# The same calls in another order: the hand-written programs of a pipelined decoder-layer kernel, permuted on all five engines

## The chip, the cores and the metric

The kernel runs on 1 core of one Trainium2 chip. The metric is the device time of one execution in microseconds (us). Before, the median of 3 runs was 291.18 us (291.09 to 291.26). The core has four compute engines and a queue engine: TensorE (PE; its weight loads are shown as PEld), VectorE (DVE), ScalarE (ACT), GpSimd (POOL) and SyncE (SP), which issues nearly all of the DMAs. Each works through its own list of instructions in order; between engines there are only semaphores.

## The reference, cut to what matters

A decoder layer over `x` (16 batches x 128 rows x 256) and a context (16 x 128 x 64). `ln` is layer normalisation without parameters, `bf` rounds to bf16, `mx` rounds each block of 32 values to 8 bits with a shared power of two.

```
q, k, v = x @ Wq.T, x @ Wk.T, x @ Wv.T
x1 = ln(x + (q * cumsum(k * v, rows) * sqrt(256)/128) @ Wo.T)

scores = q_head(x1) . k_head(ctx) / sqrt(8)      # 32 query heads over 8 key heads, 8 wide
x2 = ln(x1 + softmax(scores) @ v_head(ctx))      # keys and values are the context itself

xb = bf(x2)
h  = bf(ln(xb) * ln_w + ln_b)
h  = bf(mx(h) @ mx(W1).T + b1)                   # 256 -> 1024
h  = bf(gelu_tanh(h))
h  = bf(mx(h) @ mx(W2).T + b2)                   # 1024 -> 256
out = ln(x2 + bf(xb + h))
```

## The kernel before

The 16 batches are 8 pairs, p = 0 to 7; `b` is the batch within a pair. A pair goes through seven stages, and at any time several pairs are under way, each in another stage: p[0] to p[6] in the code are the pairs in stages 0 to 6.

- Stage 1: `kv_proj`, `q_proj` (from `xt_r`, the transposed input that POOL rounds and splits in `split_xt_high` and `split_xt_low`), `k_times_v`, `running_sum`, `out_proj`, then `residual1`, `moments`, `mean_var` and a normalisation to x1.
- Stages 2 and 3, attention, where most of the time goes. `x1T` transposes x1 on PE, and ACT copies it to `xT`. POOL's `keys(p, b, u)` spreads the context keys over the heads (`kbd`, 96 x 512 each). `scores_a(p, b, k)`, k = 0 to 7, are PE matmuls whose only use is the row maximum, which DVE's `maxima(p, b, k)` takes (a reduction of a 128 x 512 PSUM bank, L1343). `max_high`, `max_low`, PE's `maxT`, and a small DMA by SP (`max_rows`, `xT<-mT`, L399) bring the maxima into `xT` as extra rows. `scores_b(p, b, k)` (L2175) makes the scores again with the maximum taken off, ACT's `exps` (L878) exponentiates them, `weigh` (L2188) multiplies with the values, `denominators` and `attention` on DVE and `residual2` on POOL end it.
- Stage 4: `norm3` (DVE, L1381), `weight3` and `shift3` (POOL, L595 and L601), then `quantise_h(p, 0)` to `(p, 6)` (DVE, L1431 to L1444), `h_T`, `ffn_up`, `hidden`, `gelu`, and `quantise_g(p, b, 0)` to `(p, b, 9)` (DVE).
- Stages 5 and 6: `g_T` (PE, L2241), `ffn_down` (L2254), `ffn_out` and `residual3` (POOL, L607 and L614), the last norm and the store.

Each engine has one program made of three functions written by hand: `head()` (pairs 0 to 3 started, and the weights of the FFN quantised by `weight_maxima`, `weight_scales` and `quantise_weight` on DVE), `step(p, on)`, which is run four times with the seven stages on seven pairs, and `tail()`. The order of the calls in them is the only thing that sets the order on an engine. Each call waits on semaphores for its inputs and for its output buffer. The waits are counts, so they don't change when a call moves.

Two waits matter below. `keys(p, b, 0)` writes over what the pair before read, and so it waits for that pair's last `scores_b` of the same batch; `keys(p, b, 1)` behind it has no wait of its own:

```
                if later(p) and u == 0:
                    pool.wait_ge(s_sbm, 16 * (p - 1) + 8 * (b + 1))
```

And SP's `load_xt(1)` waits until DVE has used the first block (`sp.wait_ge(s_lo0, 1)`). `warm`, `warm_p` and `warm_last` on PE are matmuls of zeros (L2026) whose result nobody reads. Where a group of calls such as the norm of the last stage appears with a last argument 0 or 1, it is one batch of the pair.

Of the kernel before, what the change touches and what calls it, by code (L numbers as in the profile page):

```python
# [45 lines left out]
def decoder_kernel(nc: bass.Bass, x, xt, ctx3, ctxv, wkv, wq, wo, ln_wb, w1, bias, w2, tri, ident, diag, out):  # L46
# [17 lines left out]
    with ExitStack() as ctx:  # L64
# [286 lines left out]
        def _(sp):  # L351
# [54 lines left out]
            def head():  # L406
                load_xt(0)
                load_weight("diag")
                load_weight("ident")
                load_weight("tri")  # L410
                load_values(0)
                load_weight("wo")
                load_keys(0)
                load_xt(1)
                load_weight("w1")
                load_x(0)
                load_bias()
                load_weight("ln")
                load_weight("w2")
                load_values(1)  # L420
                load_x(1)
                load_xt(2)
                load_keys(1)
                load_keys(2)
                load_x(2)
                load_xt(3)
                load_values(2)
                max_rows(1, 0)
                max_rows(1, 1)
                load_x(3)  # L430
                load_keys(3)
                spread_bias()
                load_xt(4)
                max_rows(2, 0)
                load_values(3)
                load_keys(4)

            def step(p, on):
                if on[3]:
                    max_rows(p[3], 1)  # L440
                if on[0]:
                    load_xt(p[0])
                if on[1]:
                    load_x(p[1])
                    load_values(p[1])
                if on[2]:
                    max_rows(p[2], 0)
                if on[5]:
                    store(p[5])
                if on[0]:  # L450
                    load_keys(p[0])
# [16 lines left out]
        def _(pool):  # L468
# [148 lines left out]
            def head():  # L617
                values(0)
                keys_rounded(0)
                split_xt_high(1)  # L620
                split_xt_low(1)
                keys(0, 0, 0)
                keys(0, 0, 1)
                var_eps(0, mv1, ve1, s_mv1, s_ve1, 0)
                rstd(0, ve1, rs1, s_ve1, s_rs1, 0)
                split_xt_high(2)
                split_xt_low(2)
                keys(0, 1, 0)
                var_eps(0, mv1, ve1, s_mv1, s_ve1, 1)
                rstd(0, ve1, rs1, s_ve1, s_rs1, 1)  # L630
                keys(0, 1, 1)
                keys_rounded(1)
                var_eps(1, mv1, ve1, s_mv1, s_ve1)
                rstd(1, ve1, rs1, s_ve1, s_rs1)
                shift_product(1, mv1, rs1, nb1, s_rs1, s_nb1)
                shift(1 - 1, nb1, s_nb1)
                split_xt_high(3)
                split_x1_high(1, 0)
                split_x1_high(1, 1)
                split_x1_low(1)  # L640
                split_xt_low(3)
                split_bias()
                keys(1, 0, 0)
                keys(1, 0, 1)
                keys(1, 1, 0)
                var_eps(2, mv1, ve1, s_mv1, s_ve1)
                rstd(2, ve1, rs1, s_ve1, s_rs1)
                values(1)
                keys(1, 1, 1)
                shift_product(2, mv1, rs1, nb1, s_rs1, s_nb1)  # L650
                shift(2 - 1, nb1, s_nb1)
                residual2(0)
                split_x1_high(2, 0)
                split_x1_high(2, 1)
# [3 lines left out]
                shift(0, nb2, s_nb2)  # L658
                keys_rounded(2)
# [3 lines left out]
                weight3(0)  # L663
                keys(2, 0, 0)
                shift3(0)
                keys(2, 0, 1)
                split_xt_high(4)
                keys(2, 1, 0)
                keys(2, 1, 1)
                keys_rounded(3)  # L670
                values(2)
                split_xt_low(4)

            def step(p, on):
# [4 lines left out]
                if on[6]:  # L679
                    shift_product(p[6], mv4, rs4, nb4, s_rs4, s_nb4)  # L680
                    shift(p[6], nb4, s_nb4)
# [2100 lines left out]
```

## Time and profile before

| | |
|---|---|
| median of 3 runs | 291.18 us (291.09 to 291.26) |
| profiled execution, its own time | 292.19 us |
| its span, first to last instruction | 290.4 us |
| mean granted TensorE clock | 0.982 |
| head, first row maximum at | 21.45 us |
| the four steps, about | 84.7 to 203.0 us |
| tail, about | 203.0 to 290.4 us |

All stretches and starts below are from that one profiled execution. A timeline row gives the start, the busy time, the engine, the line, the operation with its output and inputs, how many instructions it stands for, and in brackets how long the engine had been idle and what released it. Consecutive rows of an engine may overlap a little, since one instruction starts before the last has ended.

### The profile page before, as it was taken

The numbers are of one execution on the slowest core, as the hardware profiler recorded it, in microseconds if no ns is written. First come the engines' busy times: TensorE is split into PE (matmuls) and PEld (weight loads), VectorE is DVE, ScalarE is ACT, GpSimd is POOL, SyncE is SP. The second block draws the span as 40 slices with busy tenths as digits, with TensorE's granted clock in tenths as the row PEclk, the third lists the DMA queues.
The fourth block names the chain that finished last, engine by engine and source line by source line (L and its number), as shares of the span: only waits on it lengthen the run. The fifth ranks groups of instructions, "written<-read, shape, count | busy, mean of one in ns | idle before, by whom it ended". The sixth has DMA issues, their size and how long they took to land.

```text
span 290.4 us, 5342 instructions
## 1 busy us (share of the span) xinstructions
PE 271.7 (94%) x1640; PEld 165.5 (57%) x1640; DVE 256.2 (88%) x678; ACT 226.4 (78%) x386; POOL 174.6 (60%) x253
## 2 busy tenths in 40 slices
PE   7899998999998999999989998999699989997799
PEld 3776755476565775667556756575346444543354
DVE  3489899996999799999999999989996998799982
ACT  5551768479997699988998899889998899875650
POOL 2737291687466687868786878667777353533321
PEclk9999999999997999999999999999959999999999
DMA  7930200002110020022002200210010000100111
GB/s 238 393 113 2 99 3 0 10 5 71 37 43 0 0 79 15 2 65 77 11 5 64 79 9 5 67 43 9 7 36 5 2 1 0 37 2 1 38 37 38
DMA packets 11053, 12.68 MB, mean 44 GB/s; under 512 B 3216, under 2 KB 8336, under 8 KB 10768
## 3 DMA queue, kind: packets, MB, share of 16 engines
q1 hardware_dynamic: 10592, 11.55, 12.5%
q10 hardware_dynamic: 432, 0.79, 0.7%
q8 instruction: 13, 0.21, 0.3%
q14 instruction: 16, 0.13, 0.2%
HBM read 9.84 MB, written 2.10 MB: 41 GB/s over the span
## 4 chain that ended last, share of the span: by engine, by line
PE 55%; DVE 25%; ACT 7%; issue 6%; POOL 3%; DMA 3%; DVEq 0%; POOLq 0%; ACTq 0%
PE bank L2141 8%; PE bank L2175 8%; PE bank L2188 5%; DVE nm L1343 5%; PE bank L2075 4%; PE bank L2026 3%; PE bank L2062 3%; PE bank L2254 3%; PE bank L2101 3%; DVE st L1298 3%; PE bank L2229 2%; PE bank L2088 2%; PE bank L2125 2%; PE bank L2196 2%; DMA xT<-mT 2%
## 5 line engine op out<-in xcount | busy, mean ns | idle before, releaser
L1343 DVE TENSOR_REDUCE nm<-bank 128x4 f32<-128x512 f32 x128 | 84.0, 678 | 3.0 <-PE bank L2141 2.6
L878 ACT ACTIVATE p_sb<-bank 128x512 f32<-128x512 f32 x128 | 72.2, 600 | 11.1 <-PE bank L2175 10.5
L2141 PE MATMUL bank<-kbd,xT 96*128 96x512 f32 x128 | 56.2, 470 | 2.2 <-ACT xT L849 1.5
L2175 PE MATMUL bank<-xT,kbd 104*128 104x512 f32 x128 | 53.4, 448 | 4.6 <-DMA xT<-mT 3.1
L557 POOL TENSOR_TENSOR kbd<-k3r,diag_sb 96x512 fp32r<-96x512 f32 x32 | 33.5, 1061 | 11.4 <-PE bank L2175 11.4
L2175 PEld LDWEIGHTS bank<-xT,kbd 104*128 104x128 f32 x128 | 24.7, 194 | 18.1 <-ACT p_sb L878 5.9
L2141 PEld LDWEIGHTS bank<-kbd,xT 96*128 96x128 f32 x128 | 24.6, 195 | 16.4 <-DVE nm L1343 9.3
L2188 PE MATMUL bank<-p_sb,va_sb 128*32 128x512 f32 x256 | 33.7, 616 | 0.0
L511 POOL TENSOR_TENSOR rs<-ve,nhalf 128x2 f32<-128x2 f32 (+1 forms) x36 | 26.1, 724 | 4.6
L506 POOL TENSOR_SCALAR ve<-mv 128x2 f32<-128x2 f32 (+1 forms) x36 | 8.4, 233 | 33.4 <-DVE mv L1304 31.7
L2062 PE MATMUL bank<-wkv_r,xt_r 128*128 128x512 f32 x84 | 23.7, 404 | 0.0
L892 ACT ACTIVATE y_sb<-bank 128x512 bf16<-128x512 f32 x32 | 19.1, 596 | 5.5 <-PE bank L2229 4.8
L849 ACT ACTIVATE xT<-bank 96x512 fp32r<-96x512 f32 x32 | 18.6, 585 | 5.5 <-PE bank L2125 5.4
L1298 DVE BATCH_NORM_STATS2 st<-r_sb 128x6 f32<-128x256 f32 x48 | 19.3, 416 | 0.6 <-POOL r_sb L614 0.3
L2125 PEld LDWEIGHTS bank<-idr,x 128*96 128x96 f32 x128 | 14.2, 164 | 9.5 <-DVE nm L1343 3.6
L2229 PE MATMUL bank<-w1T,hT 128*128 128x512 bf16 x64 | 19.1, 379 | 0.0
L2026 PE MATMUL bank<-zero_b 128*128 128x512 bf16 x80 | 18.9, 379 | 0.0
L902 ACT ACTIVATE gT<-bank 128x1024 bf16<-128x1024 bf16 x16 | 16.3, 1022 | 2.9 <-PE bank L2241 2.8
L607 POOL TENSOR_TENSOR s_sb<-y_sb,xb_all 128x512 bf16<-128x512 bf16 x7 | 8.3, 1183 | 16.8 <-ACT y_sb L933 16.8
L2125 PE MATMUL bank<-idr,x 128*96 128x128 f32 x128 | 17.5, 260 | 0.5 <-ACT xT L871 0.5
L2062 PEld LDWEIGHTS bank<-wkv_r,xt_r 128*128 128x128 f32 x84 | 15.7, 189 | 3.5 <-issue 0.3
L898 ACT ACTIVATE g_sb<-y_sb 128x1024 bf16<-128x1024 bf16 x16 | 16.9, 1057 | 0.4
(135 smaller groups left out, 619.6 us busy)
## 6 DMA issues: line engine op xcount, KB each, us to landing
xt_sb<-in_xt SPq DMA_DIRECT2D x8, 256.0 KB, 2.9
x_sb<-in_x SPq DMA_DIRECT2D x8, 256.0 KB, 2.9
out_dram<-o_sb SPq DMA_DIRECT2D x7, 256.0 KB, 2.2
k_sb<-in_ctx SPq DMA_DIRECT2D x8, 192.0 KB, 2.9
x_all<-in_w SPq DMA_DIRECT2D x1, 1024.0 KB, 5.2
w_raw<-in_w SPq DMA_DIRECT2D x1, 1024.0 KB, 7.3
p_sb<-in_wkv ACTq DMA_DIRECT2D x2, 256.0 KB, 4.1
cv_sb<-in_ctxv SPq DMA_DIRECT2D x8, 64.0 KB, 2.0
```

The lines of the kernel that those rows point to most:

```text
L511: gp.tensor_tensor(rs[:, part(b)], ve[:, part(b)], nhalf[:, part(b)], ALU.pow).then_inc(rs_ready, batches(b))
L557: gp.tensor_tensor(kbd[0:MR, b, u, :, :], k3r[:, b, u, :].bitcast(F32).unsqueeze(1).to_broadcast([MR, KU, P]), diag_sb[0:MR, :].unsqueeze( ...
L878: sc.activation(p_sb[:, k, :], bankB[k % 2][:, :], ACT.Exp, scale=SCORE_SCALE).then_inc(s_ex, 1)
L1298: ve.bn_stats(st[:, b, :], rows).then_inc(st_ready, 1)
L1343: ve.tensor_reduce(nm[:, b, u, g, :], bankA[(2 + k + 11 * b) % 2][:, :].rearrange("p (k t) -> p k t", k=KU), AX.X, ALU.max, negate=True).t ...
L2026: mm(bankB[0][:, :], zero_b[:, 0:P], zero_b[:, :], start=True, stop=True)
L2062: last = mm(bankP[b][:, :], xt_r[:, a, c, b, :], wkv_r[:, w, c, :], start=c == 0 and n == 0, stop=c == KC - 1 and n == len(PARTS) - 1)
L2125: last = mm(bk[0:MR, g * P:(g + 1) * P], x3[:, b, u, g, :, :].rearrange("p a r -> p (a r)"), idr[:, :], start=True, stop=True)
L2141: mm(bankA[(2 + k + 11 * b) % 2][:, :], xT[0:MR, b, u, g, :], kbd[0:MR, b, u, :, :].rearrange("r k t -> r (k t)"), start=True, stop=True). ...
L2175: mm(bankB[k % 2][:, :], kbd[0:MR + 2 * KU, b, u, kk, :], xT[0:MR + 2 * KU, b, u, :, :].rearrange("r g s -> r (g s)"), start=True, stop=Tr ...
L2188: last = mm(value_bank(p, b)[VW * k:VW * (k + 1), :], va_sb[:, at0:at0 + VW], p_sb[:, u * KU + k, :], start=u == 0, stop=u == U - 1, tile_ ...
L2229: last = mm(bk[:, :], hT[:, c, b, :], w1T[:, c, cols], start=False, stop=c == KC - 1)
```

## The change

Every engine's `head()`, `step()` and `tail()` contain the same calls as before, with the same arguments, in another order. Nothing else differs, but that the line numbers of the helpers move by a few (POOL's by 1, ACT's by 6, PE's by 4). The number of calls is (head, step, tail) SP 30, 7, 6; POOL 55, 30, 63; ACT 100, 45, 92; DVE 187, 75, 189; PE 168, 62, 162. The head is reordered from its first call on; the step in some ten places; the tail mostly in its first third and around the last pairs.

The diff, cut to what the prediction speaks of:

```diff
@@ SP, head @@
                 load_xt(0)
+                load_bias()
                 load_weight("diag")
+                load_keys(0)
+                load_x(0)
+                load_weight("wo")
+                load_xt(1)
                 load_weight("ident")
                 load_weight("tri")
+                load_weight("w2")
+                load_weight("w1")
...
@@ POOL, head @@
                 weight3(0)
+                shift3(0)
                 keys(2, 0, 0)
-                shift3(0)
...
@@ POOL, step @@
                     weight3(p[4])
+                if on[2]:
+                    keys(p[2], 0, 0)
+                if on[4]:
                     shift3(p[4])
                 if on[2]:
-                    keys(p[2], 0, 0)
                     keys(p[2], 0, 1)
+                if on[0]:
+                    split_xt_high(p[0])
                 if on[5]:
                     ffn_out(p[5])
                     residual3(p[5])
                 if on[0]:
-                    split_xt_high(p[0])
                     split_xt_low(p[0])
...
@@ ACT, head @@
                 first_high(2)
+                first_high(3)
+                v_copy(0, 0)
+                identities()
+                q_copy(0)
+                v_copy(0, 1)
                 diagonal_rows(0)
-                first_high(3)
-                identities()
-                v_copy(0, 0)
-                v_copy(0, 1)
-                q_copy(0)
+                weight_magnitudes(1)
+                v_copy(1, 0)
                 weight_magnitudes(0)
...
                 gelu(0, 1)
+                x1T(2, 1, 0)
+                x1T(2, 1, 1)
                 exps(2, 0, 0)
                 exps(2, 0, 1)
-                norm1(3, 0)
                 v_copy(4, 0)
                 exps(2, 0, 2)
-                x1T(2, 1, 1)
+                norm1(3, 0)
...
@@ DVE, head @@
                 k_times_v(0, 0)
+                q_times_sum(0, 0)
                 k_times_v(0, 1)
-                q_times_sum(0, 0)
+                residual1(0, 0)
+                moments(0, 0, r1_sb[:, 0, :], st1, s_r1, 2 * 0 + 1, s_st1)
+                mean_var(0, 0, st1, mv1, s_st1, s_mv1)
                 q_times_sum(0, 1)
-                residual1(0, 0)
+                weight_maxima(1, 0)
...
@@ DVE, step @@
                     maxima(p[3], 1, 5)
+                if on[4]:
+                    norm3(p[4], 0)
+                    norm3(p[4], 1)
                 if on[5]:
                     quantise_g(p[5], 1, 9)
-                if on[4]:
-                    norm3(p[4], 0)
-                    norm3(p[4], 1)
...
                     quantise_h(p[4], 1)
+                if on[3]:
+                    denominators(p[3], 0)
+                if on[4]:
                     quantise_h(p[4], 2)
...
-                if on[3]:
-                    denominators(p[3], 0)
...
@@ DVE, tail @@
-                quantise_g(4, 1, 9)
...
                 norm3(5, 1)
+                quantise_g(4, 1, 9)
                 quantise_h(5, 0)
@@ PE, step @@
                 if on[1]:
                     kv_proj(p[1], 1, 0)
                 if on[3]:
-                    scores_b(p[3], 0, 1)
+                    scores_a(p[3], 1, 1)
+                    scores_b(p[3], 0, 0)
+                    scores_a(p[3], 1, 2)
...
                     scores_a(p[3], 1, 6)
+                if on[1]:
+                    q_proj(p[1], 1)
+                if on[3]:
                     scores_a(p[3], 1, 7)
                     scores_b(p[3], 0, 7)
                 if on[5]:
                     g_T(p[5], 1)
-                if on[1]:
-                    q_proj(p[1], 1)
...
@@ PE, tail @@
                 scores_b(7, 1, 0)
+                g_T(5, 1)
+                values_back(7, 0)
+                scores_b(7, 1, 1)
...
```

**POOL in a step, from `weight3(p[4])` on.** `h_sb` is the FFN's normalised input, `kbd` the spread keys, `xt_r` the rounded input of pair p[0], `s_sb` and `r_sb` are `ffn_out` and `residual3`. Before:

```order
L595 TENSOR_TENSOR h_sb<-h_sb,lnwb_sb 128x512
L601 TENSOR_TENSOR h_sb<-h_sb,lnwb_sb 128x512
L557 TENSOR_TENSOR kbd<-k3r,diag_sb 96x512 x2
L607 TENSOR_TENSOR s_sb<-y_sb,xb_all 128x512
L614 TENSOR_TENSOR r_sb<-x_all,s_sb 128x512
L528 TENSOR_SCALAR xt_r<-xt_sb 128x512
L533 TENSOR_TENSOR xt_r<-xt_sb,xt_r 128x512
```

The same place after the change:

```order
L596 TENSOR_TENSOR h_sb<-h_sb,lnwb_sb 128x512
L558 TENSOR_TENSOR kbd<-k3r,diag_sb 96x512
L602 TENSOR_TENSOR h_sb<-h_sb,lnwb_sb 128x512
L558 TENSOR_TENSOR kbd<-k3r,diag_sb 96x512
L529 TENSOR_SCALAR xt_r<-xt_sb 128x512
L608 TENSOR_TENSOR s_sb<-y_sb,xb_all 128x512
L615 TENSOR_TENSOR r_sb<-x_all,s_sb 128x512
L534 TENSOR_TENSOR xt_r<-xt_sb,xt_r 128x512
```

One of the two `keys` now stands ahead of `shift3`, on which DVE's `quantise_h` waits, and `split_xt_high` stands ahead of `ffn_out`.

**PE near the end of the tail, from `g_T(7, 0)` on.** `gq` is the quantised hidden layer, `w2T` and `gT` the operands of `ffn_down`, `bias_h` its bias row, and the matmuls out of `zero_b` are the fillers. Before:

```order
L2241 MATMUL bank<-idb,gq 128x128 x8
L2026 MATMUL bank<-zero_b 128x512 x14
L2252 MATMUL bank<-bias_h,ones_b 128x256
L2254 MATMUL bank<-w2T,gT 128x256 x8
L2026 MATMUL bank<-zero_b 128x512 x6
L2241 MATMUL bank<-idb,gq 128x128 x8
L2026 MATMUL bank<-zero_b 128x512 x4
L2252 MATMUL bank<-bias_h,ones_b 128x256
L2254 MATMUL bank<-w2T,gT 128x256 x8
```

The same place after the change:

```order
L2245 MATMUL bank<-idb,gq 128x128 x8
L2030 MATMUL bank<-zero_b 128x512 x8
L2256 MATMUL bank<-bias_h,ones_b 128x256
L2258 MATMUL bank<-w2T,gT 128x256 x8
L2030 MATMUL bank<-zero_b 128x512 x10
L2245 MATMUL bank<-idb,gq 128x128 x8
L2030 MATMUL bank<-zero_b 128x512 x6
L2256 MATMUL bank<-bias_h,ones_b 128x256
L2258 MATMUL bank<-w2T,gT 128x256 x8
```

The same 24 fillers stand there, six fewer ahead of the first `ffn_down` and four and two more ahead of what follows.

## Rows read from the trace of the kernel before

**Rows 1.** windows of steps and tail: busy PE, PEld, DVE, ACT, POOL; clock; DMA share; GB/s

```profile
84.70:203.00 118.30, 113.41 (x710) 73.92 (x711) 113.10 (x297) 104.49 (x185) 87.08 (x120) 0.99 0.12 34
203.00:290.40 87.40, 78.91 (x468) 39.72 (x466) 72.92 (x214) 65.10 (x104) 38.25 (x62) 0.96 0.05 17
```

**Rows 2.** the page: the chain that ended last, by engine

```profile
PE 55%; DVE 25%; ACT 7%; issue 6%; POOL 3%; DMA 3%; DVEq 0%; POOLq 0%; ACTq 0%
```

**Rows 3.** timeline of DVE, 13 to 22 us

```profile
14.00 2.00 DVE L1263 TENSOR_TENSOR gz<-gz 128x1024 bf16<-128x1024 bf16 x2
...
21.45 0.69 DVE L1343 TENSOR_REDUCE nm<-bank 128x4 f32<-128x512 f32 x1 [0.41 <-PE bank L2141]
```

**Rows 4.** timeline of ACT and of SP's queue, 0 to 13 us

```profile
2.10 0.43 SPq L394 DMA_DIRECT2D tri_sb<-in_tri  x1
...
5.86 0.35 SPq L358 DMA_DIRECT2D xt_sb<-in_xt  x1
...
6.17 1.14 ACT L841 ACTIVATE kbd<-diag_sb 32x512 fp32r<-32x512 f32 x2
```

**Rows 5.** timeline of DVE and POOL around 42 us

```profile
41.16 0.67 DVE L1285 TENSOR_TENSOR wz<-w_raw,win 128x512 int16<-128x512 f32 x1
41.75 2.81 DVE L1285 TENSOR_TENSOR wz<-x_all,win 128x512 int16<-128x512 f32 x1
...
41.99 2.02 POOL L557 TENSOR_TENSOR kbd<-k3r,diag_sb 96x512 fp32r<-96x512 f32 x2
```

**Rows 6.** timeline of DVE, `quantise_h` of pair 0 and of pair 5

```profile
71.10 0.69 DVE L1431 TENSOR_REDUCE am<-h_sb 128x16 f32<-128x512 bf16 x1 [2.16 <-POOL h_sb L601]
...
220.06 0.69 DVE L1431 TENSOR_REDUCE am<-h_sb 128x16 f32<-128x512 bf16 x1 [2.87 <-POOL h_sb L601]
```

**Rows 7.** timeline of PE at the entry to the steps, then its stretch

```profile
89.52 0.73 PE L2141 MATMUL bank<-kbd,xT 96*128 96x512 f32 x2 [1.45 <-ACT xT L849]
...
90.00:93.40 3.40, 3.40 (x20) 2.96 (x18) 3.40 (x9) 2.04 (x5) 3.01 (x6) 0.56 0.00 0
...
95.66 0.69 DVE L1343 TENSOR_REDUCE nm<-bank 128x4 f32<-128x512 f32 x1 [0.97 <-PE bank L2141]
```

**Rows 8.** timeline of PE in the third step

```profile
146.15 0.50 PE L2175 MATMUL bank<-xT,kbd 104*128 104x512 f32 x1 [0.66 <-DMA xT<-mT]
```

**Rows 9.** timeline of POOL, 156 to 167 us

```profile
156.94 1.28 POOL L595 TENSOR_TENSOR h_sb<-h_sb,lnwb_sb 128x512 f32<-128x512 f32 x1 [1.38 <-DVE h_sb L1381]
...
159.67 2.04 POOL L557 TENSOR_TENSOR kbd<-k3r,diag_sb 96x512 fp32r<-96x512 f32 x2
162.77 1.16 POOL L607 TENSOR_TENSOR s_sb<-y_sb,xb_all 128x512 bf16<-128x512 bf16 x1 [1.06 <-ACT y_sb L933]
```

**Rows 10.** timeline of DVE, 159 to 167 us; the last row in the tail

```profile
159.74 0.69 DVE L1431 TENSOR_REDUCE am<-h_sb 128x16 f32<-128x512 bf16 x1 [0.55 <-POOL h_sb L601]
...
160.77 0.96 DVE L1436 TENSOR_SCALAR sc<-am 128x16 bf16<-128x16 f32 x1
...
163.25 0.96 DVE L1444 TENSOR_TENSOR hq<-z,sc 128x512 bf16<-128x512 bf16 x1
...
166.19 0.42 DVE L1298 BATCH_NORM_STATS2 st<-r_sb 128x6 f32<-128x256 f32 x1
166.71 0.18 DVE L1304 BATCH_NORM_AGGREGATE mv<-st 128x2 f32<-128x6 f32 x1
...
249.48 0.17 DVE L1436 TENSOR_SCALAR sc<-am 128x16 bf16<-128x16 f32 x1
```

**Rows 11.** timeline of DVE and PE, 247 to 282 us

```profile
247.97 0.36 DVE L1361 RECIPROCAL rden<-bank 128x32 f32<-128x32 f32 x1 [2.29 <-PE bank L2196]
...
276.36 3.18 PE L2026 MATMUL bank<-zero_b 128*128 128x512 bf16 x14
...
280.27 0.69 DVE L1444 TENSOR_TENSOR gq<-gz,sc 128x1024 bf16<-128x1024 bf16 x1
...
281.66 0.61 PE L2241 MATMUL bank<-idb,gq 128*128 128x128 bf16 x8
```

More of the change, by code:

```diff
@@ L1055, in step @@
                     norm4(p[6], 1)
+                if on[3]:
+                    exps(p[3], 0, 5)
+                if on[5]:
+                    gT_copy(p[5], 0)
                 if on[3]:
@@ L1706, in step @@
                     norm3(p[4], 1)
+                if on[5]:
+                    quantise_g(p[5], 1, 9)
                 if on[3]:
@@ L1857, in tail @@
                 attention(6, 1, 1)
+                mean_var(4, 1, st4, mv4, s_st4, s_mv4)
                 quantise_g(5, 0, 2)
@@ L1975, in tail @@
                 quantise_g(7, 0, 9)
+                quantise_g(7, 1, 0)
+                quantise_g(7, 1, 1)
                 moments(6, 0, r3_sb[:, 0, :], st4, s_r3, 2 * 6 + 1, s_st4)
[L1977 to L1981 removed]
                 quantise_g(7, 1, 2)
@@ L2450, in step @@
                 if on[3]:
-                    scores_b(p[3], 0, 0)
+                    scores_a(p[3], 1, 0)
+                    x1T(p[3], 1, 1)
                 if on[1]:
@@ L2478, in step @@
                 if on[3]:
+                    scores_a(p[3], 1, 5)
+                    scores_b(p[3], 0, 5)
+                    scores_b(p[3], 0, 6)
+                    weigh(p[3], 0, 0)
                     scores_a(p[3], 1, 6)
+                if on[1]:
+                    q_proj(p[1], 1)
+                if on[3]:
                     scores_a(p[3], 1, 7)
@@ L2501, in step @@
                     scores_a(p[2], 0, 0)
+                    scores_a(p[2], 0, 1)
                 if on[3]:
@@ L2626, in tail @@
                 scores_b(7, 0, 5)
-                scores_a(7, 1, 7)
+                warm_p(2)
                 scores_b(7, 0, 6)
                 warm_p(2)
+                scores_a(7, 1, 7)
+                warm_p(2)
                 scores_b(7, 0, 7)
+                g_T(5, 0)
                 weigh(7, 0, 0)
+                warm_p(2)
                 maxT(7, 1)
-                warm_p(2)
-                g_T(5, 0)
                 weigh(7, 0, 1)
                 scores_b(7, 1, 0)
+                g_T(5, 1)
+                values_back(7, 0)
+                scores_b(7, 1, 1)
                 warm_p(2)
-                scores_b(7, 1, 1)
-                g_T(5, 1)
                 scores_b(7, 1, 2)
-                warm_p(2)
+                ffn_down(5, 1)
                 scores_b(7, 1, 3)
-                values_back(7, 0)
-                ffn_down(5, 1)
                 scores_b(7, 1, 4)
+                ffn_down(5, 0)
                 scores_b(7, 1, 5)
-                ffn_down(5, 0)
+                weigh(7, 1, 0)
+                h_T(6)
                 scores_b(7, 1, 6)
```

756 lines of the change are left out of this document (360 added, 396 removed).

## The prediction

> **What bounds the kernel now.** I read the windows first. In the four steps PE is busy 113.41 of 118.30 us and DVE 113.10, so the two share the bound and neither has 5 us to give; ACT and POOL have slack. In the tail PE is busy 78.91 of 87.40 us, part of it fillers, and DVE only 72.92 [rows 1]. The chain says the same in another way: 55% of the span is PE, 25% DVE, 7% ACT, and 6% "issue" [rows 2]. An order can't make the busy time shorter (no instruction is removed), only the waits. So I went through the timelines of PE and DVE for idle time whose releaser is another engine, and through DVE for instructions that last longer than their like. Then I laid the new order over the measured times and asked at each such place what stands there now.
>
> **The change part by part.** The sum is made against the profiled execution's own time, 292.19 us, which is 1.01 above the median of 291.18; the difference is taken over to the median.
>
> *Start, to the first row maximum at 21.45 us [rows 3].* Before, DVE runs two `weight_maxima` in 2.00 us (from 14.00) ahead of the first `moments`; now `residual1`, `moments` and `mean_var` stand in front of them. ACT's two `diagonal_rows` instructions cost 1.14 us at 6.17 [rows 4] and stood ahead of the last rounding of the query weights; now one call is behind the copies and the other far back. The gain can't be the full 2.00 + 1.14, since the first `keys` and x1's transposes must be there too: I put it at 1.05 us, near the middle. Against it works SP: `tri` was issued at 2.10, and is now behind `load_xt(1)`, which waits for DVE and was issued at 5.86 [rows 4]; with one issue (0.43) between, and two to three us for landing, `tri` is there at about 9.6, where `running_sum(0)` would want it at about 10.4 if PE and DVE gain what is said above; both are my estimates. Bounds: -1.4 (everything follows) to +1.0 (`tri` is late).
>
> *A held instruction at 42 us.* One `quantise_weight` on DVE takes 2.81 us, while its neighbour of the same form takes 0.67; it ends with POOL's two `keys` (41.99, 2.02) [rows 5]. In the new order another instruction meets them. I take -0.5; the bounds are -2.1 (2.81 less 0.67) and +0.5. In the head six more DVE instructions than before stand right behind the one whose result they need; in a step such a pair leaves 0.10 us between its two (166.19 + 0.42 to 166.71) [rows 10], where others overlap slightly. 6 x 0.12 is 0.7 at most; +0.4, since some fall into waits.
>
> *`quantise_h(0, 0)`* waits 2.16 us for POOL [rows 6]. `shift3(0)` is now ahead of `keys(2, 0, 0)`. Part of it only moves the wait: -0.4 (0 to -1.0, one `keys`, half of the 2.04 in rows 9).
>
> *Entry to the steps.* ACT copied x1's last transpose behind three `exps`, so PE stood idle 1.45 us; right after it the granted clock was 0.56 from 90.00 to 93.40, that is mostly at 1.2 GHz instead of 2.4, and DVE then waited 0.97 us for PE [rows 7]. ACT now makes that copy first. I take -1.0, the size of DVE's wait; the bounds are 0 and -1.5.
>
> *The steps, four times.* (a) `denominators(p[3], 0)` moves among the first instructions of `quantise_h`, into a stretch whose end is set by POOL. (b) Three dependent pairs fewer, 3 x 0.12. (c) `scores_b(0, 0)` is now behind one more `scores_a`, so the wait of 0.66 us for the small DMA [rows 8] becomes about 0.35. (d) `norm3` is 0.6 us sooner, with `quantise_g(p[5], 1, 9)` behind it. (e) Against: one `keys`, 1.02 us (half of 2.04) stands ahead of `shift3`, so `quantise_h(0)`, which already waited 0.55 [rows 10], starts about 1.0 - 0.6 = 0.4 later. That costs nothing if `quantise_h` was being held up anyway: `L1436` takes 0.96 us against 0.17 when POOL is quiet, and `L1444` 0.96, which ends as POOL's `ffn_out` does (162.77 + 1.16 = 163.93) [rows 9, 10]; and `ffn_out` waits for ACT, not for DVE. Without this cover it costs 0.4 a step. Sum a step: 0.27 + 0.36 + 0.3 = 0.93 at most of which waits elsewhere eat a part; (b) and (c) lie on different engines and only the later one counts. I take -0.4 a step, -1.6 in all; bounds 0 and -2.6.
>
> A rule bears on (e) and on the 42 us. The Trainium skill, page "SBUF — State Buffer", section "Who interferes with whom", says that VectorE and GpSimd share one pair of ports as an exclusive lock: a VectorE copy or tensor_scalar in a fast mode, or one with two inputs in SBUF, stands still until the GpSimd instruction ends, and a reduction never does. The rows agree (2.81 against 0.67, 0.96 against 0.17 us). By that rule `split_xt_high`, which the change puts just ahead of `ffn_out`, can also hold one of `quantise_h`'s instructions, by less than its own length; counted in full that would make the steps' term about zero instead of -1.6.
>
> *Tail.* The wait of 2.87 us ahead of `quantise_h(5, 0)` [rows 6] now has `quantise_g(4, 1, 9)` in it, about -0.6, but the `mean_var` of stage 4 is later, +0.35. At 247.97 DVE waited 2.29 us for PE's `values_back(7, 0)` [rows 11], which now stands directly behind `g_T(5, 1)`: -0.85, as the wait for the other batch behind it stays. Near the end 14 fillers take 3.18 us, 0.23 each, ahead of `ffn_down(7, 0)`; now 8, and 10 where 6 were. `g_T(7, 1)` started at 281.66, 0.70 us after its input was ready (280.27 + 0.69) [rows 11]; the fillers ahead of it are now 18 where there were 20, so -0.4 to -0.7. Together -1.5; bounds -3 and +0.5.
>
> *What I did not see.* Nearly every call of the head moved, and waits of 0.5 to 1.5 us as at the entry appear wherever two engines' orders don't match. I allow +1.5.
>
> Sum: -1.05 - 0.5 + 0.4 - 0.4 - 1.0 - 1.6 - 1.5 + 1.5 = -4.15. On 292.19 that gives 288.0, and on the median 287.0 us.
>
> **The rivals.**
>
> A, the forecast: gains in all three parts, 287.0 us, own range 284.0 to 289.5.
>
> B: the steps don't gain. PE is busy 96% of them [rows 1], and what DVE saves it then waits for PE. For it: both engines are full, so a gain must come on both. Against: the 0.66 of rows 8 is on PE. Time: 287.0 + 1.6 = 288.6.
>
> C: everything found is given back by mismatched waits in the head, so that it ends at 291.2: the allowance would be 5.7 instead of 1.5, four waits like the 1.45 of rows 7. The port rule above, counted in full, gives 288.6 alone and so is in B.
>
> D, slower. In a step POOL's `keys(p[2], 0, 0)` waits for the last `scores_b(p[3], 0)` of PE, and `shift3` is now queued behind it, and with it DVE's `quantise_h`, and behind that `h_T` and the FFN. In the new order that `scores_b` stands behind `q_proj(p[1], 1)`, later than before. Measured POOL comes to it at 156.94 + 1.28 = 158.2; I reckon PE's last `scores_b` about 0.7 us after it was, just in time. Each us that it is later passes to DVE four times. From 4.15 / 4 = 1.05 us a step on it decides; at 1.5 us the kernel takes 287.0 + 6 = 293.0. For it: POOL's `keys` had no one waiting behind them before, PE has no slack in the steps. Against: DVE's stretch there has 0.79 us of held time to absorb.
>
> **How the numbers follow.** A has 0.54, B 0.20, C 0.08 and D 0.18. The predicted time is that of A, 287.0. The range goes down to 284.0, where start, entry, steps and tail come near their lower bounds together (about 0.07 below it), and up to 292.5, which takes in B, C and the milder half of D. A measurement of this kernel can tell about 0.2%, 0.58 us, from no change. Faster by more: A and B with a little of C, 0.75; within: most of C, 0.07; slower: 0.18.
>
> **What would show it.** In the new profile: first row maximum at about 20.4 us; no idle time of PE of over 1 us at the entry to the steps and no clock below 0.9 there; the same row of successive steps 29.2 us apart or less (118.30 / 4 = 29.6 now [rows 1]); DVE's wait for `h_sb` in a step below 1 us, and POOL not idle ahead of the first `keys` (if it waits there for PE over a us, D is right); the wait for `xT<-mT` on PE halved; at the end `g_T(7, 1)` sooner after its input. The prediction is wrong if the steps are longer apart than before, if `tri` holds up the first `running_sum`, or if the head shows new waits for SP's loads, which have changed places the most.

## The result: 6.4% slower, and the profile after

The changed kernel takes 310.29 us (median of 4 runs, 308.89 to 310.97) beside 291.22 us before (4 runs): 1.064 times as long, 95% interval 1.059 to 1.069. I had forecast 287.0 us. The profiled execution has a span of 308.2 us (290.4 before) and a mean clock of 0.961 (0.982).

Page of the changed kernel, busy time, its slices and the chain that ended last:

```profile
PE 280.2 (91%) x1640; PEld 169.8 (55%) x1640; DVE 264.1 (86%) x678; ACT 226.6 (74%) x386; POOL 177.6 (58%) x253
...
PEclk9999999999999799989999799979967999999999
...
PE 42%; DVE 35%; issue 10%; ACT 6%; POOL 3%; DMA 2%; ACTq 0%; DVEq 0%; POOLq 0%
```

The same instructions are busy 7.9 us longer on DVE and 8.5 on PE (256.2 and 271.7 us before). On the chain that ended last, PE has lost about what DVE and "issue" have won [rows 2]. So there are not only new waits: some instructions on DVE last longer than they did. The view that finds them is the groups of instructions by line. Of DVE in the changed kernel (count, busy us, mean ns of one, idle us before them):

```profile
L1353 DVE CAST mx<-nm 128x32 bf16<-128x32 f32 x12 | 12.0, 1002 | 0.2
L1357 DVE TENSOR_TENSOR mx<-nm,mx 128x32 bf16<-128x32 f32 x12 | 6.7, 560 | 0.2
```

The same two groups of the kernel before:

```profile
L1354 DVE TENSOR_TENSOR mx<-nm,mx 128x32 bf16<-128x32 f32 x12 | 3.6, 298 | 0.2
L1350 DVE CAST mx<-nm 128x32 bf16<-128x32 f32 x12 | 3.0, 254 | 0.2
```

These are `max_high` and `max_low`, tiny instructions that I had not looked at. Together they take 18.7 us in place of 6.6. These 12.1 us are more than the 7.9 that DVE is busier, so some other instructions became shorter. PE's `maxT` waits for them. An instruction that lasts longer than others of its shape, because another engine is at work, is called held below. Windows of the changed kernel, the steps and then one place in the second step (columns as in [rows 1]):

```profile
84.70:220.80 136.10, 121.73 (x717) 77.58 (x717) 122.81 (x303) 104.92 (x185) 88.74 (x120) 0.95 0.10 30
...
134.00:137.00 3.00, 0.52 (x5) 0.38 (x6) 2.96 (x3) 0.28 (x1) 2.76 (x3) 0.93 0.02 5
137.00:140.00 3.00, 3.00 (x16) 2.50 (x16) 1.19 (x3) 1.24 (x3) 0.00 (x0) 0.50 0.04 11
```

The place itself, timelines of POOL, DVE and PE, and at the end two equal groups of `ffn_down` on PE:

```profile
131.36 1.59 POOL L596 TENSOR_TENSOR h_sb<-h_sb,lnwb_sb 128x512 f32<-128x512 f32 x1 [0.92 <-DVE h_sb L1384]
132.91 1.03 POOL L558 TENSOR_TENSOR kbd<-k3r,diag_sb 96x512 fp32r<-96x512 f32 x1
133.91 1.26 POOL L602 TENSOR_TENSOR h_sb<-h_sb,lnwb_sb 128x512 bf16<-128x512 f32 x1
135.14 1.03 POOL L558 TENSOR_TENSOR kbd<-k3r,diag_sb 96x512 fp32r<-96x512 f32 x1
...
133.05 3.21 DVE L1353 CAST mx<-nm 128x32 bf16<-128x32 f32 x1
136.30 0.60 DVE L1357 TENSOR_TENSOR mx<-nm,mx 128x32 bf16<-128x32 f32 x1
...
140.09 0.36 DVE L1364 RECIPROCAL rden<-bank 128x32 f32<-128x32 f32 x1 [1.87 <-PE bank L2200]
...
136.96 0.32 PE L2157 MATMUL bank<-idb,mx 128*72 128x128 bf16 x1 [2.48 <-DVE mx L1357]
137.29 1.92 PE L2258 MATMUL bank<-w2T,gT 128*128 128x256 bf16 x8
...
140.37 1.04 PE L2258 MATMUL bank<-w2T,gT 128*128 128x256 bf16 x8
```

Read it from the top. `keys` (132.91) follows `weight3` (131.36 + 1.59 = 132.95) without a pause, then `shift3`, then the second `keys`. DVE's `max_high` comes at 133.05, finds POOL at work, and lasts 3.21 us, to the end of the third POOL instruction; in the other three steps it lasts 2.21 or 2.22, to the end of the second. PE waits 2.48 us for `maxT` (1.9 in the others), and behind `maxT` stand `ffn_down`, `values_back` and all the scores. Right after that wait the granted clock is 0.50 (1.2 GHz) for 3 us, and DVE's `denominators` waits 1.87 us for the `values_back` that is late. The steps are 33.9 us apart instead of 29.6.

The clock has a share of its own. It falls after the wait in the other three steps too (windows of the changed kernel):

```profile
100.00:104.00 4.00, 2.11 (x15) 1.38 (x12) 3.90 (x5) 1.56 (x5) 3.08 (x4) 0.81 0.00 0
168.00:174.00 6.00, 4.10 (x26) 3.30 (x22) 4.12 (x7) 1.77 (x5) 3.00 (x4) 0.73 0.02 5
203.00:210.00 7.00, 5.55 (x32) 4.77 (x33) 4.57 (x12) 3.10 (x7) 1.24 (x2) 0.76 0.02 5
```

Eight matmuls of `ffn_down` take 1.92 us at 137.29 and 1.04 at 140.37, when the clock is back. PE's four waits for `maxT`, 1.89, 2.48, 1.90 and 1.90 us, are 8.2 us, and PE's extra busy time over the whole span is 8.5 us. My estimate from these two sums is that about half of what the steps lost is the wait and half the slower PE behind it; no run divides them.

Where the 19 us are, by DVE's starts in both traces: the first `max_high` of a step is 0.55 us later than before, the last one (233.13 in place of 216.06, in the first part of the tail) 17.1, and the last `quantise_g` 18.3. That gives the head, the steps (with the first part of the tail) and the rest of the tail some 0.6, 16.5 and 1.2 us; the last stretch to the end of the span is 0.5 us shorter. The two spans differ by 17.8 us, the two medians by 19.1.

### The profile page after: what moved, and what is told of

Its sections match the earlier page's. It is cut to its first block, busy times and chain, and to the rows that moved or that the text cites. A ratio compares the mean times of both kernels' runs of the same rounds, so it can differ in the third digit from the quotient of the medians.

```text
span 308.2 us, 5342 instructions
## 1 busy us (share of the span) xinstructions
PE 280.2 (91%) x1640; PEld 169.8 (55%) x1640; DVE 264.1 (86%) x678; ACT 226.6 (74%) x386; POOL 177.6 (58%) x253
## 4 chain that ended last, share of the span: by engine, by line
PE 42%; DVE 35%; issue 10%; ACT 6%; POOL 3%; DMA 2%; ACTq 0%; DVEq 0%; POOLq 0%
PE bank L2179 6%; PE bank L2145 6%; DVE nm L1346 5%; PE bank L2258 4%; DVE mx L1353 3%; DVE st L1301 3%; PE bank L2105 3%; PE bank L2066 3%; DVE gq L1447 2%; PE bank L2079 2%; PE bank L2192 2%; DVE gz L1490 2%; DVE gz L1443 2%; DMA p_sb<-in_wq 2%; PE bank L2233 2%
## 5 line engine op out<-in xcount | busy, mean ns | idle before, releaser
L2179 PE MATMUL bank<-xT,kbd 104*128 104x512 f32 x128 | 54.1, 458 | 1.1 <-ACT p_sb L884 0.9
L558 POOL TENSOR_TENSOR kbd<-k3r,diag_sb 96x512 fp32r<-96x512 f32 x32 | 34.0, 1072 | 12.4 <-PE bank L2179 12.1
L2192 PE MATMUL bank<-p_sb,va_sb 128*32 128x512 f32 x256 | 34.7, 627 | 1.0 <-ACT p_sb L884 0.9
L507 POOL TENSOR_SCALAR ve<-mv 128x2 f32<-128x2 f32 (+1 forms) x36 | 9.4, 262 | 38.4 <-DVE mv L1307 37.2
L2066 PE MATMUL bank<-wkv_r,xt_r 128*128 128x512 f32 x84 | 24.7, 410 | 1.1 <-DVE r_sb L1324 1.1
L898 ACT ACTIVATE y_sb<-bank 128x512 bf16<-128x512 f32 x32 | 19.1, 596 | 4.2 <-PE bank L2233 3.4
L2258 PE MATMUL bank<-w2T,gT 128*128 128x256 bf16 x128 | 20.0, 309 | 0.0
L2129 PEld LDWEIGHTS bank<-idr,x 128*96 128x96 f32 x128 | 15.4, 175 | 6.9 <-issue 4.7
L2233 PE MATMUL bank<-w1T,hT 128*128 128x512 bf16 x64 | 19.1, 379 | 0.0
L2030 PE MATMUL bank<-zero_b 128*128 128x512 bf16 x80 | 19.1, 379 | 0.0
```

The source lines that it names most:

```text
L558: gp.tensor_tensor(kbd[0:MR, b, u, :, :], k3r[:, b, u, :].bitcast(F32).unsqueeze(1).to_broadcast([MR, KU, P]), diag_sb[0:MR, :].unsqueeze( ...
L2066: last = mm(bankP[b][:, :], xt_r[:, a, c, b, :], wkv_r[:, w, c, :], start=c == 0 and n == 0, stop=c == KC - 1 and n == len(PARTS) - 1)
L2129: last = mm(bk[0:MR, g * P:(g + 1) * P], x3[:, b, u, g, :, :].rearrange("p a r -> p (a r)"), idr[:, :], start=True, stop=True)
L2179: mm(bankB[k % 2][:, :], kbd[0:MR + 2 * KU, b, u, kk, :], xT[0:MR + 2 * KU, b, u, :, :].rearrange("r g s -> r (g s)"), start=True, stop=Tr ...
L2192: last = mm(value_bank(p, b)[VW * k:VW * (k + 1), :], va_sb[:, at0:at0 + VW], p_sb[:, u * KU + k, :], start=u == 0, stop=u == U - 1, tile_ ...
L2233: last = mm(bk[:, :], hT[:, c, b, :], w1T[:, c, cols], start=False, stop=c == KC - 1)
```

## The experiments

Each ratio is against the kernel before on the same chip, and the brackets are its 95% interval. The kernel before took 291.0 to 292.0 us on these chips, so a difference of under 1 us between times from two chips says little. "Apart" is the distance of `max_high(p, 1)` from step to step in the profile, (start in the fourth - start in the first) / 3: 29.59 us before, 33.91 after.

**One call put back in the changed kernel** (POOL, step):

```diff
                     weight3(p[4])
-                if on[2]:
-                    keys(p[2], 0, 0)
-                if on[4]:
                     shift3(p[4])
                 if on[2]:
+                    keys(p[2], 0, 0)
                     keys(p[2], 0, 1)
```

> The changed kernel with one call put back: in the step, POOL's keys(p[2], 0, 0) behind shift3 again. Theory G (gap): the two dependent POOL calls weight3 and shift3 left 0.15 us between them, in which DVE's max_high got the shared ports; with keys between them POOL's train has no gap, max_high lasts 2.2 to 3.2 us instead of 0.3 and PE waits 1.9 to 2.5 us for it, in each of four steps. Then about 10 us come back (2.5 x 4): 300 us, and max_high lasts 0.3 us. Theory N (norm3 earlier): POOL's calls now meet max_high because norm3 was moved ahead of quantise_g; then keys alone gives back one keys (1.0 us) x 4: 306 us, and max_high still lasts over 1 us. Theory D (denominators): the wait of 1.8 us for PE in front of the rest of quantise_h is the cost; then this run stays at 309 to 310 us.

Measured: 296.87 us (1.017, 1.015 to 1.020), 30.46 apart. `max_high` lasts 0.24 us again. One call of 1.03 us is 13.4 of the 19 us, more than the 10 us of theory G; theory N's 306 us and theory D's 309 are out. The clock is back as well: PE's 717 matmuls of the steps are busy 115.79 us at a clock of 1.00 (window 84.7 to 207.0 us), where the same number took 121.73 at 0.95 in the changed kernel. So some 6 us of the 13.4 may be PE's speed. Timelines of DVE and POOL in this run:

```profile
129.82 0.24 DVE L1351 CAST mx<-nm 128x32 bf16<-128x32 f32 x1
130.10 1.20 DVE L1355 TENSOR_TENSOR mx<-nm,mx 128x32 bf16<-128x32 f32 x1
...
128.14 1.59 POOL L596 TENSOR_TENSOR h_sb<-h_sb,lnwb_sb 128x512 f32<-128x512 f32 x1 [0.92 <-DVE h_sb L1382]
129.87 1.28 POOL L602 TENSOR_TENSOR h_sb<-h_sb,lnwb_sb 128x512 bf16<-128x512 f32 x1
```

`shift3` depends on `weight3`, so there are 0.14 us between them, and `max_high` slips in. `max_low` does not: it is held 1.20 us.

**`denominators(p[3], 0)` put back** on DVE behind `maxima(p[2], 0, 1)`, alone and with `keys`:

```diff
                     quantise_h(p[4], 1)
-                if on[3]:
-                    denominators(p[3], 0)
...
                     maxima(p[2], 0, 1)
+                if on[3]:
+                    denominators(p[3], 0)
```

> The changed kernel with denominators(p[3], 0) on DVE put back behind maxima(p[2], 0, 1) in the step. Theory D: 1.8 us x 4 come back, and a little for the clock: 302 to 303 us. Theory G: max_high is still held 2.2 us or more, and the wait of denominators was only PE's lateness after it; quantise_h goes on during PE's catching up, so 1 to 4 us come back: 306 to 309 us. Theory N: like G.

> Both of these put back in the changed kernel. Theory G: as with keys alone within 1 us, about 299 to 300 us, if the wait of denominators follows from max_high. If both have a price of their own, 10 + 7 less than 310: 293 us. Theory N: about 302 us.

Measured: 309.84 us (1.064, 1.061 to 1.067) and 297.74 (1.021, 1.019 to 1.024). The wait of `denominators`, 1.5 to 1.9 us in each step, is real, and taking it away gives back nothing that can be told: it is PE's lateness seen from DVE. Theory D falls. The 1 to 4 us that theory G expected back in the first of the two runs did not come either.

**The kernel before with one call moved** (`keys(p[2], 0, 0)` between `weight3` and `shift3`, nothing else):

> The kernel before with one call moved: in the step, POOL's keys(p[2], 0, 0) between weight3 and shift3. Theory G: max_high is held 2 us or more here too, PE waits for it: 291.2 + 8 to 10 = 299 to 301 us. Theory N (norm3 must be earlier for it): max_high comes when weight3 has just ended, keys holds it by 1.0 us at most, quantise_h starts 1 us later of which the held time takes most: 291 to 295 us. Theory D: 291 to 292 us.

Measured: 297.72 us (1.024, 1.021 to 1.028), 31.35 apart, between theory N's 291 to 295 and theory G's 299 to 301. Here `max_high` gets in and `max_low` is the one that is held, to the end of `shift3` (130.14 + 1.26):

```profile
128.99 0.30 DVE L1352 CAST mx<-nm 128x32 bf16<-128x32 f32 x1
129.32 2.24 DVE L1356 TENSOR_TENSOR mx<-nm,mx 128x32 bf16<-128x32 f32 x1
...
127.90 1.28 POOL L595 TENSOR_TENSOR h_sb<-h_sb,lnwb_sb 128x512 f32<-128x512 f32 x1 [1.38 <-DVE h_sb L1383]
129.14 1.04 POOL L557 TENSOR_TENSOR kbd<-k3r,diag_sb 96x512 fp32r<-96x512 f32 x1
130.14 1.26 POOL L601 TENSOR_TENSOR h_sb<-h_sb,lnwb_sb 128x512 bf16<-128x512 f32 x1
131.36 1.04 POOL L557 TENSOR_TENSOR kbd<-k3r,diag_sb 96x512 fp32r<-96x512 f32 x1
```

So the move alone costs 6.2 us without any of the other edits, a third of the whole; within the change it costs twice as much. `max_high` got in here although there is no pause: `weight3` ended at 129.18 and `keys` started at 129.14. DVE's instruction started at 128.99, while `weight3` still ran; in the changed kernel it started 0.14 us after `keys`.

**The order of the change, with the pause given back**: one wait for `weight3` in front of `keys(p[2], 0, 0)`.

> The changed kernel, order untouched, with one wait added: in the step POOL's keys(p[2], 0, 0) first waits until weight3 has ended, as shift3 did when it stood there. No order changes; only the 0.1 to 0.2 us between the two instructions come back. Theory G (it is the gap through which DVE's max_high and max_low took the shared ports): max_high, which is ready 0.1 us after weight3's end, gets in and lasts 0.3 us; max_low may be held by keys or not; at least half of what putting keys back gave (13.4 us) comes back: 297 to 304 us. Theory L (length: DVE meets any POOL instruction that runs then, and it is the keys instruction, 1.03 us, ahead of shift3 that costs): nothing comes back, 309 to 311 us.

Measured: 310.21 us, `max_high` 2.3 to 3.3 us. My expectation was wrong, and the trace of it says why:

```profile
132.08 1.03 POOL L558 TENSOR_TENSOR kbd<-k3r,diag_sb 96x512 fp32r<-96x512 f32 x1
...
132.10 3.33 DVE L1354 CAST mx<-nm 128x32 bf16<-128x32 f32 x1
```

`keys` now starts 0.08 us behind `weight3` (it ended at 132.00), and DVE's instruction starts 0.02 us after it. Whether a pause alone is enough stays open; what the run does show is that an added wait on POOL gives nothing while `max_high` is held. The next run took the overlap away altogether.

**The order of the change, with `keys` waiting for DVE's `max_low`:**

```diff
                 if on[2]:
+                    pool.wait_ge(s_ml, 2 * p[2])
                     keys(p[2], 0, 0)
```

> The changed kernel, order untouched, with one more wait: in the step POOL's keys(p[2], 0, 0) waits for DVE's max_low(p[3], 1). The run before showed that the gap behind weight3 comes back (0.08 us) but DVE's max_high was ready 0.02 us after keys had started, so it said little on the mechanism. Theory T (train: max_high, once it finds POOL at work on keys, is held to the end of two or three POOL instructions, since they follow each other without a pause, and PE waits for its result): here max_high and max_low find POOL standing, last 0.3 us each, PE's wait is gone, keys starts 0.7 us later than now, and most of the 13.4 us comes back: 296 to 300 us, though keys still stands ahead of shift3. Theory L (the cost is the 1.03 us of keys, and now 0.7 more, ahead of shift3 and so of quantise_h, h_T and the FFN; this was my rival D's consequence): 310 to 313 us.

Measured: 300.83 us (1.031, 1.026 to 1.036), 31.60 apart: an added wait makes the kernel 9.5 us faster. That is 0.8 us outside theory T's range and far from theory L's 310 to 313; of L's mechanism a smaller part is there. (The profiled execution was the fastest of five, 298.05 us.)

```profile
129.44 0.24 DVE L1354 CAST mx<-nm 128x32 bf16<-128x32 f32 x1
129.72 0.31 DVE L1358 TENSOR_TENSOR mx<-nm,mx 128x32 bf16<-128x32 f32 x1
...
130.10 1.04 POOL L558 TENSOR_TENSOR kbd<-k3r,diag_sb 96x512 fp32r<-96x512 f32 x1 [0.77 <-DVE mx L1358]
...
132.40 0.69 DVE L1435 TENSOR_REDUCE am<-h_sb 128x16 f32<-128x512 bf16 x1 [0.90 <-POOL h_sb L602]
```

Neither of the two is held, and what is left of the move is the plain queueing of `shift3` behind `keys`, with the 0.77 us that `keys` itself now waits: `quantise_h` waits 0.90 us where it waited for nothing in the changed kernel. By these runs a step has 33.91 - 31.60 = 2.3 us of holding, with the late and slower PE behind it. 31.60 - 30.46 = 1.1 us is queueing together with the added wait, which no run divides, and 30.46 - 29.59 = 0.9 us is something else.

**That something else**, with keys and denominators put back. First DVE's `norm3` behind `quantise_g(p[5], 1, 9)` again, as before the change:

> The changed kernel with keys and denominators put back (297.7 us before this) and with DVE's norm3 behind quantise_g(p[5], 1, 9) again in the step. With keys put back, max_low is still held 1.20 us by shift3 where it took 0.30 before the change, since norm3, and so weight3, is 0.7 us earlier and its end no longer meets max_high. Theory N2 (that costs the remaining 0.8 us a step): max_low takes 0.3 us and 3 us come back, 294.5 to 295 us. Rival P (the remaining 0.8 us a step are from PE's new order): no change, 297 to 298 us, though max_low is short again.

Measured: 296.66 us, 30.35 apart: `max_low` is short again (0.31), and 0.3 us a step come back (30.64 apart with only keys and denominators put back) of the 0.8 expected. The time lies outside both ranges. What stays is a wait on DVE:

```profile
DVE vh_sb L1315 <- ACT q_sb L862: 3.6, 4, 0.9
```

(four waits of 0.9 us of `q_times_sum` for ACT's `q_copy`). PE's whole step put back to the old order on top of it:

> The kernel of the run with keys, denominators and norm3 put back (296.7 us), with PE's step put back to the order of before as well; ACT, SP and the rest stay as in the changed kernel. There residual1 waits 0.6 us in each step, and the steps are 0.55 us longer than before. Theory P (PE's new order, with x1T(p[2], 1, 0) behind values_back, and scores_b(0, 7) later, costs it): steps 29.6 us again, 2 us less, 294.3 to 295 us. If it is ACT's order or denominators and DVE's other moves: 296 to 297 us.

Measured: 298.85 us (1.025, 1.019 to 1.031), 31.11 apart: worse, and outside both expectations. I read it so that PE's new order fits ACT's new order, and that one engine's old order among the others' new ones loses more than it gives; no run tests that reading. Then only `q_proj(p[1], 1)` behind `scores_b(p[3], 0, 7)` and `g_T(p[5], 1)` again, and the same move made in the kernel before:

> The kernel with keys, denominators and norm3 put back (296.7 us), and on PE in the step q_proj(p[1], 1) behind scores_b(p[3], 0, 7) and g_T(p[5], 1) again. In the trace of that kernel DVE's q_times_sum waits 0.90 us for ACT's q_copy, which stands behind the last exps and gT_copy, and these wait for scores_b(0, 7), which is 1.1 us later since q_proj is ahead of it. Theory Q (that one call): the wait of q_times_sum goes, steps are 29.6 to 29.8 us apart instead of 30.3, and 2 to 3 us come back: 293.7 to 294.7 us. Rival M (many small mismatches): 296 to 297 us.

> The kernel before with that one move alone: on PE in the step q_proj(p[1], 1) ahead of scores_a(p[3], 1, 7). Theory Q: scores_b(0, 7) is 0.9 us later, with it the last exps, gT_copy and q_copy on ACT and q_times_sum on DVE, and the steps are 0.6 us longer: 293 to 294.5 us. Rival M: 291 to 292 us.

Measured: 295.84 us, 30.18 apart, and 291.55 us (0.999, 0.997 to 1.002), 29.80 apart. The wait goes from 0.9 to 0.17 us and appears at 0.56 us in the other kernel, as theory Q says, but a step moves by 0.2 us only. Theory Q is right on the wait and wrong on its price (295.84 lies between its range and rival M's, 291.55 in rival M's). This call is a small part, and the remaining 0.6 us a step are not settled.

**Whole functions.** The changed kernel with the step of all five engines from before, and the kernel before with the new head alone:

> The changed kernel with the step of all five engines from before; the new head and tail stay. Theory S (the loss is in the step alone): steps 29.6 us apart; the head's end is 0 to 1.2 us later than before, the tail within 1.5 us: 290 to 294 us. If the rest of the 5 us that is left after keys comes from head and tail by themselves: 296 us.

> The kernel before with the head of all engines from the changed one; step and tail from before. My sum had -2.5 us for the head with the entry to the steps. In the changed kernel the first row maximum was 0.4 us earlier, but the first quantise_g 1.25 us later than before. If the head's gain is lost in its last part: 291 to 293 us. If the old step takes up what the head gives (the entry without the 1.45 us wait on PE): 289 to 290 us.

Measured: 294.34 us (1.009, 1.006 to 1.012), 29.60 apart, and 292.99 us (1.004, 1.001 to 1.006). By these medians the step has 16 of the 19 us, the head about 1, the tail about 1.4; the steps are 29.60 us apart again, as before the change.

**Terms of my sum by themselves.** ACT's `x1T(2, 1, 1)` early and the fillers 4, 5, 3:

> The kernel before with two of the change's edits by themselves, at two places far apart: ACT's copy x1T(2, 1, 1) directly behind gelu(0, 1) in the head (my entry term, -1.0), and at the end 4, 5 and 3 fillers where 7, 3 and 2 stood, as in the changed kernel (my filler term, -0.4 to -0.7; here 9 ahead of g_T(7, 1) where 10 were). If the entry term is right, the 1.45 us wait of PE at 89.5 us is gone and max_high(2, 1) comes 0.5 to 1.0 us sooner than 98.83; if the fillers are right, the last quantise_g to the end of the span is 0.2 us or more shorter. Both: 289.8 to 290.4 us. If what the entry gives is taken by the next wait: 291.

Measured: 290.91 us (0.998, 0.996 to 1.001), no change that can be told. `max_high(2, 1)` started at 98.95 (98.83 before, and the first row maximum was 0.11 later already): the entry gave nothing. PE's 1.45 us there became these two waits, and the clock from 90.00 to 93.40 was 0.60, as low as the 0.56 of [rows 7]:

```profile
89.76 0.62 PE L2241 MATMUL bank<-idb,gq 128*128 128x128 bf16 x8 [0.62 <-DVE gq L1444]
90.69 1.65 PE L2075 MATMUL bank<-xt_r,wq_r 128*128 128x256 f32 x6 [0.32 <-DVE kv_sb L1308]
```

The fillers did give something: last `quantise_g` to the end of the span went from 10.1 to 9.7 us. Then `shift3(0)` ahead of `keys(2, 0, 0)`, with 4, 3 and 2 fillers and three more at the very end:

> The kernel before with two small edits: in the head POOL's shift3(0) ahead of keys(2, 0, 0), and at the end 4, 3 and 2 fillers where 7, 3 and 2 stood, the other three behind ffn_down(7, 1). The fillers: g_T(7, 1) no longer waits behind them (it started 0.70 us after its input), so the end comes 0.5 to 0.7 us sooner against the last quantise_g. shift3: if DVE's wait of 2.16 us ahead of quantise_h(0, 0) is on the path, that call and all behind it come 0.7 to 1.0 us sooner, and the whole is 289.6 to 290.0 us; if only DVE's slack grows, the first quantise_g stays where it is and the whole is 290.5.

Measured: 292.24 us (1.003, 1.001 to 1.005), slower by a little, and outside both expectations. `quantise_h(0, 0)` came 1.02 us sooner and `maxima(2, 0, 0)` 0.04: DVE had slack there, the term is nothing. And something else now set the end of the span: DVE's last result came at 286.40 (288.09 before), PE's last filler at 289.76 (290.15 before). PE, then DVE:

```profile
282.69 7.07 PE L2026 MATMUL bank<-zero_b 128*128 128x512 bf16 x32
...
285.99 0.41 DVE L1421 TENSOR_SCALAR o_sb<-r_sb,mv,rs 128x256 f32<-128x256 f32 x1 [1.06 <-POOL rs L511]
```

The store that follows DVE's last result takes about 2.2 us, so it would be over at 288.6, and the fillers end at 289.76 of 290.0. So eight of the 16 closing filler calls were left out (nobody reads their result):

> The kernel with the two small edits (shift3(0) ahead of keys(2, 0, 0), three fillers moved behind ffn_down(7, 1)), and 8 of the 16 closing fillers left out (work whose result nobody reads). In that kernel PE's last filler ended at 289.76 of a span of 290.0, while DVE ended at 286.40 and the store behind it takes about 2.2 us. If the closing fillers set the end, the span is now set by the store, 1.2 to 1.4 us sooner: 290.9 us, or 0.1 to 0.7 us less than before. If the store or something else set it, nothing changes: 292.2 us.

Measured: 290.50 us, beside 291.35 before on that chip (0.997, 0.995 to 0.999): 0.3% faster than before and 6% faster than the change, the only kernel here whose interval lies below that of no change. It does less work than either, by the eight filler calls.

## Why the prediction was wrong, point by point

- **The step that failed is (e) of the steps' sum**: with one `keys` ahead of `shift3`, `quantise_h(0)` starts 0.4 us later, and "That costs nothing if `quantise_h` was being held up anyway". The sum took -1.6 us for the four steps; measured, they lost about 16. I followed the moved call to the DVE call that waits for its result, and not to the DVE calls that run at the same time. It set POOL's instructions one behind the other just when `max_high` and `max_low` come, which stand ahead of `quantise_h` and feed PE. This is shown by one call put back (-13.4 us), and by the wait that takes the overlap away and leaves the order (-9.5 us). In the kernel before, `max_high` (158.03) and `max_low` (158.35) passed where POOL's `weight3` had ended (156.94 + 1.28 = 158.22 [rows 9]) and `shift3`, which needs its result, had not begun (158.37). I first took this pause of 0.15 us for the cause. What the runs show is when `max_high` got in with `keys` close behind `weight3`: it did when it started 0.15 us ahead of `keys` (the run with one call moved), and not when it started 0.02 or 0.14 us after.
- **The rule was named and used on the wrong instructions.** I had the page "SBUF — State Buffer" of the Trainium skill, section "Who interferes with whom", in the text, and applied it to `quantise_h` and `split_xt_high`, not to `max_high` and `max_low` beside `keys`. By its rule a cast (`max_high`) can be held if its operands meet the conditions of a mode with two ports, and an instruction with two inputs in SBUF (`max_low`) while GpSimd reads SBUF. The rows agree: 3.21 and 1.02 us against 0.24 and 0.30. The page says that the engine that issues first has the ports for its whole instruction. Here the hold lasted over two and three POOL instructions that followed each other without a pause (2.22 and 3.21 us).
- **Rival D had the right side, and its mechanism is the smaller part.** `shift3` queued behind `keys` costs at most 1.1 us a step when `max_high` and `max_low` are not held. That PE's last `scores_b` would be late for `keys` did not happen: POOL does not wait ahead of `keys` at 132.91. I had given it 0.18 and a price from 1.05 us a step on; the real total is 4.3 us a step, and most of it was in none of my rivals. Of the cover that (e) counted on, `L1444` ended at 164.21, 0.28 after `ffn_out` (163.93), and not with it [rows 9, 10].
- **The order of events within the held stretch.** (d), `norm3` sooner, was counted as a small gain. It moved `weight3`'s end ahead of `max_high`, and cost 0.3 us a step with `keys` put back. The move of `keys` costs 6.2 us alone and 13.4 within the change; that `norm3` makes the difference is my reading of these runs, and no run tests these two edits by themselves.
- **(a) `denominators`**: not settled. With `keys` put back the kernel takes 296.87 us with the move and 297.74 without, with `keys` moved 310.29 and 309.84; in both pairs the intervals overlap. The 0.27 that my sum has for it stands on no row. **(c)** the mechanism was right: no wait for `xT<-mT` of the kind of [rows 8] is left in the changed trace; its gain is not seen, as DVE is later. **(b)**, the dependent pairs, has no run of its own.
- **Start, -1.05**: the first maximum came at 21.09 in the profile, 0.36 sooner; `tri` was not late (issued at 6.56, landed 3.1 us later, first `running_sum` at 12.16). The start scatters: it was 19.7 to 21.4 us in runs with the same head. I overlooked one more held instruction there: DVE's last rounding of the query weights (L1236) took 1.77 us at 8.09 beside POOL's preparation of the keys, and 0.69 before. It did so in four of the eleven profiles with the new head and in none with the old one; what it is worth is not shown, since the first maximum came at 21.37 in a profile without it. **42 us**: three `quantise_weight` instructions took 3.58 us from 40.91, about 1.5 more than three of 0.68; before, the held one was 2.1 too long. So the held time fell by about the -0.5 that I took, while POOL's two `keys` took 2.99 us there in place of 2.02. **`quantise_h(0, 0)`, -0.4**: its wait vanished, and by the run with `shift3(0)` moved that is worth 0.
- **Entry, -1.0**: worth 0; and in the changed kernel PE waits there again, for another copy, now behind `gelu(0, 1)`:

```profile
85.02 0.47 PE L2145 MATMUL bank<-kbd,xT 96*128 96x512 f32 x1 [1.21 <-ACT xT L855]
```

- **Tail, -1.5**: it is about 1.4 slower. The wait of 2.87 us is still 2.59 with `quantise_g(4, 1, 9)` in it, and all of it 1.2 us later, 0.4 of it from before the tail (profile of the kernel with the old step against that with the new head alone); ACT copies `x1T(7, 0, ...)` 2.1 us later in that comparison. The fillers were right: `g_T(7, 1)` now waits for its input, and no longer behind them:

```profile
299.28 0.62 PE L2245 MATMUL bank<-idb,gq 128*128 128x128 bf16 x8 [0.23 <-DVE gq L1447]
```

- **Open**: 0.6 us a step, and the parts of the 1 us of the head and the 1.4 us of the tail. Several orders together may make them; the old order of PE in the new step, which lost 2.2 us, points that way and doesn't show it. How much of the steps' loss is the lower clock is an estimate only.

## What to carry to other kernels

When a call moves, look on every engine at what runs beside it, not only at what waits for it: two tiny instructions on the path (0.25 and 0.30 us, held once a step) were worth more than any wait that I had counted. In a comparison, read the mean duration of small groups first; one that has grown while its shape has not is being held. Where the engine with slack holds short instructions of the busy one, let it wait for them: one added wait gave 9.5 us of the changed kernel back, though 3% were still missing to the kernel before.

## What the runs showed of the hardware that I had not expected

- A held DVE instruction does not get in at every boundary between two POOL instructions that follow each other at once: 2.21 to 2.33 us over one boundary, 3.21 and 3.33 over two, 1.20 with none. The pause alone does not decide which boundary lets it in. In the steps of the changed kernel, of the ones with `denominators` put back and with the first added wait, and of the kernel before with the one call moved (16 steps), the held instruction passed the boundary from `keys` to `shift3` in none, and the equally close one from `shift3` to the second `keys` in 14. In the first step of the changed kernel, for one, `shift3` ended at 101.49 and the second `keys` started at 101.46. `max_high` was done at 101.59 all the same, and `keys` then held `max_low`. Why the two boundaries differ is open. A start 0.02 us behind POOL's was late enough to be held.

```profile
99.38 2.21 DVE L1353 CAST mx<-nm 128x32 bf16<-128x32 f32 x1
101.62 1.02 DVE L1357 TENSOR_TENSOR mx<-nm,mx 128x32 bf16<-128x32 f32 x1
```

- The same wait of PE, 1.45 us at 89.5 us in the kernel before and in the one with `shift3(0)` moved, was followed by a granted clock of 0.56 in the one execution [rows 7] and not in the other (window of the latter):

```profile
90.00:93.40 3.40, 3.38 (x27) 1.99 (x26) 3.40 (x9) 3.15 (x6) 3.00 (x6) 1.00 0.00 0
```

  `max_high(2, 1)` was 1.1 us sooner in the latter, about what the profiled execution before had above its median (292.19 against 291.18). A saving of 1 us read from one profile can be this difference between two executions.
